# Spreading products for two token tiles at once, and a last norm in halves

## The chip, the cores and the metric

The kernel runs on one core of a Trainium2 chip. Its time is the device time of one execution in microseconds; several runs are taken, and their median counts.

## The reference

Two decoder layers on 1024 tokens (16 sequences of 64) of width 256. Each layer is self attention, cross attention, feed forward, each added to x and followed by a layer norm. Two places matter here. The first cross attention sees x and the context as 64 channels by 256 positions per sequence and has 8 heads of 8 channels with rotary angles:

```
q = _apply_rotary(q_emb, split_heads(_proj(x, Wq, bq)))
k = _apply_rotary(k_emb, split_heads(_proj(c, Wk, bk)))
scores = einsum('bhtc,bhsc->bhts', q, k) / sqrt(K_CH)
out = _proj(merge(einsum('bhts,bhsc->bhtc', softmax(scores), v)), Wo, bo)
```

and the very end is the last layer norm of the whole:

```
x = _layernorm(x + _L1_ffn_ref(x, ...))      # (x - mean) / sqrt(var + eps)
```

## The kernel before

All engines' instructions are written out by hand, each engine in its own program order, with semaphores between them (`wait_ge`, and `.by` to count up). x lies in SBUF as 8 tiles of 128 tokens (`NT = 8`, two sequences a tile), 256 columns each. PSUM is 8 banks of 512 columns.

**Spreading in the first cross attention.** For each tile u (0 to 7 are the keys, from the context; 8 to 15 the queries, from x) these steps follow each other:

1. `project(u)` on TensorE: one product of 256 columns into bank u % 2 (L799).
2. `rope_x(u)` on VectorE: adds the bias and multiplies with cosines and sines into `qr[:, u % 2]`, a buffer for two tiles (L2001). It waits until the spreading products of tile u-2 have read it.
3. `replicate(u)` on TensorE: spreads the 64 channels of both sequences of the tile (p = 0, 1) to 128 rows, for both halves of the heads (g = 0, 1), cosine and sine part (i = 0, 1). Each is a product of 64 rows by 128 columns, 256 columns moving, and f32, which the trace shows as two passes: 16 passes (L811). The two sequences stand in different row halves of the array.
4. `hi_part(u)` on ScalarE: two copies of a bank to f16 (L1634).
5. `stack_x(u)` on VectorE: two steps that put high and low parts into `stack`, f16 (L2009).

The bank of a product is chosen by sequence: banks 4 and 5 for all key tiles, 4 to 7 in turn for the queries. Thus for keys `replicate(u)` waits for `stack_x(u-1)`.

In the keys half TensorE also does the six large projections of the self attention (`project0`, 4 passes of 512 columns, L771) for tiles 0 to 5 and two value projections (`project_v0`, L781), and after it the value tiles of the cross attention (`values_in_x`, L826; j = 4 to 7 into banks 6 and 7, j = 0 to 3 into 4 and 5), the first scores (`scores0`, L838) and the memory products (`memory0`, L851) of the self attention. VectorE divides the latter (`memory_out0`, L2016, L2021), has the ELU steps (L2035, L2036) at tile 7, and then goes through the 16 softmax steps (L1978, L1979). ScalarE has `keep_v0` (L1645) and the bias step (L1661). After the norm of the self attention comes the queries half, with nothing but steps 1 to 5, and then the first score products (L938).

**The end.** The last feed forward runs in 16 half steps. Of each, TensorE's `outputs` sums down products into banks 4 to 7 (L1538, L1543, and, after VectorE's `down_ranks6`, L2503, the products L1547). After the last but one, tiles 0 to 3 are complete, after the last tiles 4 to 7. `take_sum(j)` adds tile j to x and takes its statistics (L2460, L1953, L1954). `normalise(6)` adds eps (L1958), waits for ScalarE's root (`ln_sqrt`, L1618), takes the reciprocal (L1960) and does 8 steps (L1962). SyncE then stores x with one DMA.

Of the kernel before, what the change touches and what calls it, by code (L numbers as in the profile page):

```python
# [13 lines left out]
ALU = mybir.AluOpType  # L14
# [3 lines left out]
P = 128  # L18
# [5 lines left out]
EPS = 1e-5  # L24
# [107 lines left out]
def build(nc, a):  # L132
    ctx = ExitStack()
    with ctx:
# [14 lines left out]
        def bank(i, n=1):  # L149
            return psum[:, i * BANK:(i + n) * BANK]  # L150
# [338 lines left out]
        sh_silu = again("sh_silu", otx_sb, B)  # L489
        mid_act = again("mid_act", elu_exp, 1)  # L490


# [29 lines left out]

        def replicated(u, p):
            return bank(4 + p if u < NT else 4 + 2 * (u % 2) + p)

# [3 lines left out]
        def _(sp):  # L529
# [72 lines left out]
            for f in range(FX):  # L602
# [13 lines left out]
                if f >= BUFS:  # L616
                    fetch_mix(f)
            sp.wait_ge(x_norm.sem, NT * 6)
            sp.dma_start(a["out"].rearrange("(j p) d -> p j d", p=P), x).then_inc(out_done.sem, 16)
            sp.wait_ge(out_done.sem, 16)  # L620

# [120 lines left out]
        def _(pe):  # L742
# [57 lines left out]

            def replicate(u):
                pe.wait_ge(qr_ready.sem, u + 1)
                for p in range(2):
                    back = 1 if u <= NT else 2
                    if u >= back:
                        pe.wait_ge(st_ready.sem, 2 * (u - back) + p + 1)
                for g in range(2):
                    for i, w in enumerate((c["rep"], c["rep_turned"])):
                        for p in range(2):
                            rows = slice(64 * p, 64 * p + 64)  # L810
                            last = pe.matmul(replicated(u, p)[:, g * D:(g + 1) * D], w[rows, g, :], qr[rows, u % 2, i, :],  # L811
                                             start=(i == 0), stop=(i == 1), tile_position=(64 * p, 0), skip_group_check=True)
                            if g == 1 and i == 1:
                                rep_ps.by(last)
# [85 lines left out]
            for j in range(NT // 2, NT):  # L900
                values_in_x(j)
            pe.wait_ge(vx_sb.sem, 1)
# [113 lines left out]
            for u in range(NT, 2 * NT + 1):  # L1016
                if u < 2 * NT:
                    project(u)
                if u > NT:
                    replicate(u - 1)  # L1020
            pe.wait_ge(st_ready.sem, 4 * NT)
# [583 lines left out]
        def _(act):  # L1605
# [22 lines left out]

            def hi_part(u):
                for p in range(2):  # L1630
                    act.wait_ge(rep_ps.sem, 2 * u + p + 1)
                    if u >= 2:
                        act.wait_ge(st_ready.sem, 2 * (u - 2) + p + 1)
                    hi_ready.by(act.activation(hi16[:, u % 2, p, :], replicated(u, p), ACT.Copy))  # L1634

# [14 lines left out]
            for u in range(NT + 1):  # L1650
                if u < 6:
                    keep_project0(u)
                if u >= 1:
                    hi_part(u - 1)
# [38 lines left out]

            for u in range(NT, 2 * NT):
                hi_part(u)

# [227 lines left out]
            for n in range(STEPS):  # L1924
                for i, (kind, src, dst) in enumerate((("g", slice(0, P), slice(0, P)),
# [4 lines left out]
                    else:  # L1930
                        act.wait_ge(sh_h.sem, sh_h.base + 2 * len(SHARED))
                    mid_act.by(act.activation(g6[dst, 2 * (n % 2) + i, :], bank(ring[(kind, 0), n] % 4)[src, :],  # L1932
                                              ACT.Silu))
            ln_sqrt(6)

        @block.vector
        def _(dve):
# [67 lines left out]
            def stack_x(u):  # L2005
                side, j = ("k", u) if u < NT else ("q", u - NT)
                for p in range(2):
                    dve.wait_ge(hi_ready.sem, 2 * u + p + 1)
                    do(dve.scalar_tensor_tensor(  # L2009
                        out=stack[side][:, 2 * j + p, :, :].rearrange("p a b -> p (a b)"), in0=hi16[:, u % 2, p, :],  # L2010
                        scalar=c["lo_" + side], in1=replicated(u, p), op0=ALU.mult, op1=ALU.add), st_ready)

# [15 lines left out]
            for u in range(NT + 1):  # L2028
                if u < NT:
                    rope_x(u)  # L2030
                if u >= 1:
                    stack_x(u - 1)
                if u == 7:
                    dve.wait_ge(elu_exp.sem, 1)
                    do(dve.tensor_scalar(sig0, sig0, 1.0, -1.0, ALU.min, ALU.add))  # L2035
                    do(dve.tensor_tensor(out=sig0, in0=q0, in1=sig0, op=ALU.max), elu_ready)  # L2036
            for m in range(2):
                memory_out0(m)
# [11 lines left out]

            for u in range(NT, 2 * NT + 1):
                if u < 2 * NT:
                    rope_x(u)
                if u > NT:
                    stack_x(u - 1)

# [452 lines left out]
            for step in range(-1, STEPS + 1):  # L2509
                if step + 1 < STEPS:  # L2510
                    inputs6(step + 1)
                if 0 <= step < STEPS:
                    hidden6(step, 0)
                if step + 1 < STEPS:
                    ranks6(step + 1)
                if 0 <= step < STEPS:
                    hidden6(step, 1)
                if step >= 1:
                    down_ranks6(step - 1)
                if step == STEPS - 1:  # L2520
                    for j in range(4):
                        take_sum(j)
            for j in range(4, NT):
                take_sum(j)
            normalise(6)

# [158 lines left out]
```

## Time and profile before

| what | us |
|---|---|
| median of 3 runs (1118.9 to 1127.76) | 1125.86 |
| the profiled execution, whole | 1121.06 |
| its span, first to last instruction | 1119.2 |
| TensorE busy | 976.2 (87%) |
| VectorE busy | 553.1 (49%) |
| ScalarE busy | 359.2 (32%) |
| mean granted TensorE clock | 0.927 |

The span is what the trace covers; 1.9 us of the execution lie around it. Matmuls are pipelined, so busy TensorE is not TensorE at its peak. PE is TensorE's matmuls, PEld its weight loads, DVE VectorE, ACT ScalarE, POOL GpSimd, SP SyncE.

### The profile page before, as it was taken

Reading aid. Unit: us, or ns where it says so; the run is one execution under the profiler, and the core shown is the slowest. Engines: PE = TensorE matmul, PEld = TensorE weight load, DVE = VectorE, ACT = ScalarE, POOL = GpSimd, SP = SyncE. Lnnn points to the kernel's source line nnn. Section 1 sums busy time; section 2 is a strip of 40 time slices with the busy share of each in tenths; the row PEclk is TensorE's granted clock in tenths of the full one; section 3 lists DMA queues with packets and bytes.
Section 4 is the critical chain, followed back from the end, with each engine's and each line's share of the span. In section 5 each row is a group of like instructions: output and inputs, shape, how many; then the busy total and the mean of one; then the engine's idle time right before and its main releaser. Section 6 shows DMA issues by size and latency. Waiting matters only on the chain.

```text
span 1119.2 us, 18944 instructions
## 1 busy us (share of the span) xinstructions
PE 976.2 (87%) x7488; PEld 610.2 (55%) x7488; DVE 553.1 (49%) x1113; ACT 359.2 (32%) x717; POOL 200.4 (18%) x241
## 2 busy tenths in 40 slices
PE   7998879997999999966773998889589999999994
PEld 4754523333478899953352667667454444444442
DVE  2699788885421111015687676457552323323325
ACT  3444246666222223322384443334211000000000
POOL 5011000000022222210037630060000111111110
PEclk9999869998899999987986999999578999999998
DMA  6000000000745555521001102030105022222001
GB/s 232 2 2 1 1 1 2 1 2 1 282 167 165 171 185 180 183 95 49 1 1 55 22 1 96 1 136 3 47 0 131 0 86 86 86 84 73 15 1 38
DMA packets 27210, 75.15 MB, mean 67 GB/s; under 512 B 9828, under 2 KB 17260, under 8 KB 21748
## 3 DMA queue, kind: packets, MB, share of 16 engines
q1 hardware_dynamic: 24916, 67.91, 18.1%
q0 software_dynamic: 2208, 6.03, 1.9%
q8 instruction: 61, 1.00, 0.4%
q14 instruction: 25, 0.20, 0.1%
HBM read 67.48 MB, written 6.46 MB: 66 GB/s over the span
## 4 chain that ended last, share of the span: by engine, by line
PE 70%; DVE 20%; issue 3%; ACT 3%; POOL 2%; DMA 2%; SPq 0%; DVEq 0%; POOLq 0%; ACTq 0%
PE psum L1513 8%; PE psum L1088 7%; PE psum L1100 7%; DVE arena L2060 4%; PE psum L811 3%; PE psum L1517 3%; PE psum L1279 3%; PE psum L1501 3%; PE psum L1543 2%; PE psum L1547 2%; PE psum L992 2%; PE psum L1479 2%; DVE arena L1979 2%; DVE arena L1978 2%; PE psum L1494 2%
## 5 line engine op out<-in xcount | busy, mean ns | idle before, releaser
L1513 PE MATMUL psum<-arena 128*128 128x512 f32 (+1 forms) x192 | 93.6, 625 | 0.5 <-DVE arena L2487 0.5
L1932 ACT ACTIVATE arena<-psum 128x512 f32<-128x512 f32 (+1 forms) x32 | 19.0, 593 | 227.3 <-PE psum L1517 227.3
L1752 ACT ACTIVATE arena<-psum,arena 128x128 f32<-128x128 f32 x184 | 52.6, 368 | 115.4 <-PE psum L1088 115.4
L2060 DVE TENSOR_REDUCE arena<-psum 128x2 f32<-128x512 f32 x128 | 82.6, 688 | 13.1 <-PE psum L938 11.0
L1088 PE MATMUL psum<-arena 128*128 128x128 f32 x736 | 86.7, 276 | 0.0
L737 POOL TENSOR_TENSOR arena<-arena 128x512 f32<-128x512 f32 (+1 forms) x32 | 40.5, 1265 | 257.2 <-ACT arena L1932 257.2
L1088 PEld LDWEIGHTS psum<-arena 128*128 128x128 f32 x736 | 84.0, 192 | 2.7 <-issue 2.7
L1100 PE MATMUL psum<-arena 128*128 x368 | 83.1, 379 | 0.0
L2207 DVE COPY arena<-psum 128x256 f32<-128x256 f32 x23 | 9.8, 425 | 136.2 <-PE psum L1073 85.8
L1729 ACT ACTIVATE arena<-psum 128x1024 f32<-128x1024 f32 x64 | 65.4, 1024 | 32.2 <-PE psum L960 29.0
L1100 PEld LDWEIGHTS psum<-arena 128*128 128x128 f32 x368 | 68.2, 190 | 8.4
L2487 DVE TENSOR_TENSOR arena<-arena,psum 128x512 f32<-128x512 f32 (+1 forms) x32 | 22.0, 688 | 90.0 <-POOL arena L737 89.5
L1513 PEld LDWEIGHTS psum<-arena 128*128 128x128 f32 (+1 forms) x192 | 34.2, 191 | 57.6 <-issue 55.9
L757 PE MATMUL psum<-arena 128*128 128x128 f32 x80 | 20.3, 401 | 44.2 <-DVE arena L1962 35.9
L938 PE MATMUL psum<-arena 32*128 32x256 f16 x256 | 47.8, 295 | 9.8 <-DVE arena L2060 4.3
L2470 DVE TENSOR_TENSOR arena<-psum,arena 128x512 f32<-128x512 f32 x32 | 22.1, 692 | 54.5 <-issue 45.8
L676 POOL DMA_INDIRECT returned<-arena x23 | 22.8, 990 | 123.1 <-DVE arena L2223 123.1
L685 POOL TENSOR_TENSOR arena<-arena 128x512 f32<-128x512 f32 x32 | 32.8, 1054 | 61.8 <-ACT arena L1792 43.7
L757 PEld LDWEIGHTS psum<-arena 128*128 128x128 f32 x80 | 11.5, 192 | 53.0 <-DVE arena L1962 40.6
L811 PE MATMUL psum<-arena 64*128 64x256 f32 x256 | 33.8, 404 | 3.8 <-DVE arena L2009 2.1
L992 PE MATMUL psum<-arena 128*32 128x256 f32 x512 | 36.0, 401 | 0.6 <-ACT arena L1729 0.5
L1517 PE MATMUL psum<-arena 64*128 64x512 f32 (+1 forms) x96 | 34.4, 625 | 0.0
(349 smaller groups left out, 1819.7 us busy)
## 6 DMA issues: line engine op xcount, KB each, us to landing
arena<-in_w SPq DMA_DIRECT2D x31, 1024.0 KB, 5.0
arena<-in_experts SPq DMA_DIRECT2D x8, 1248.0 KB, 5.9
arena<-mixed SPq DMA_DIRECT2D x16, 256.0 KB
arena<-mixed SPq DMA_DIRECT2D x8, 512.0 KB
arena<-in_ctx SPq DMA_DIRECT2D x2, 1024.0 KB, 7.1
arena<-returned SPq DMA_DIRECT2D x8, 256.0 KB, 4.6
arena<-in_w_xattn SPq DMA_DIRECT2D x1, 1538.5 KB, 10.0
arena<-in_w_ffn SPq DMA_DIRECT2D x1, 1152.0 KB, 5.2
```

What stands on the lines that cost most here:

```text
L737: do(pool.tensor_tensor(out=g6[rows, 2 * half + i, :], in0=g6[rows, 2 * half + i, :], in1=scale6[rows, f % BUFS, cols], op=ALU.mult), scaled6)
L811: last = pe.matmul(replicated(u, p)[:, g * D:(g + 1) * D], w[rows, g, :], qr[rows, u % 2, i, :], start=(i == 0), stop=(i == 1), tile_posit ...
L938: last = pe.matmul(bank(u % 2)[:, tc * D:(tc + 1) * D], stack["q"][r0:r1, b, g, tc * P:(tc + 1) * P], stack["k"][r0:r1, b, g, :], start=Tr ...
L992: last = pe.matmul(bank(6)[32 * q:32 * q + 32, 0:D], vx[:, b, sc, q, 32 * g:32 * g + 32], ptx[:, (n + q // 2) % 4, q % 2, sc, :], start=(g ...
L1088: last = pe.matmul(bank(n)[:, i * P:(i + 1) * P], w1_tile[:, r % 2, k, features], xst[:, r % 2, k, :], start=(k == 0), stop=(k == KC - 1))
L1100: last = pe.matmul(bank(4 + r % 2)[:, 0:D], hidt[:, r % 2, ic * P:(ic + 1) * P], w2v[:, bass.ds(e, 1), ic, :], start=(ic == 0), stop=(ic = ...
L1279: last = pe.matmul(bank(n % 4)[:, q * P:(q + 1) * P], lhs, xv1[rows, u, :], start=True, stop=True)
L1513: pe.matmul(out, e[w][:, k, :], xe6[:, half, k, :], start=(k == 0), stop=False)
L1517: mid_ps.by(pe.matmul(out, qb6[r0:r1, n // 2 % 2, q0:q0 + m], aw6[r0:r1, half, :], start=False, stop=True))
L1729: ptx_ready.by(act.activation(ptx[:, n % 4, :, :, :].rearrange("p a b c -> p (a b c)"), bank(2 + 2 * (n % 2), 2), ACT.Exp, scale=float(DHX ...
L1752: last = act.activation(hidt[:, r % 2, ic * P:(ic + 1) * P], bank(n)[:, i * P:(i + 1) * P], ACT.Gelu, bias=b1_tile[:, r % 4, ic:ic + 1])
L2060: ax_max.by(dve.tensor_reduce(nmx[:, b % 2, :, h], bank(u % 2).rearrange("p (t s) -> p t s", t=2), AX.X, ALU.max, negate=True))
```

## The change

The spreading products are done for two tiles at once. `replicate(m)` covers tiles 2m and 2m+1 with 512 moving columns, into bank 4 + 2g + p: four banks, by half of the heads and sequence. It runs when both tiles are roped; `rope_x(u)` of a following tile waits for the whole block before. `hi_part` and `stack_x` go by half of the heads; a stack step writes two runs of 256. All value tiles of the cross attention move behind the keys' last stack step. The last norm is done in two halves of four tiles: tiles 0 to 3 and 6, 7 are normalised on ScalarE with a scale and a shift, 4 and 5 on VectorE; `take_sum` of tiles 2 and 3 comes behind the last `down_ranks6`. The store is in three parts.

```diff
-        def replicated(u, p):
-            return bank(4 + p if u < NT else 4 + 2 * (u % 2) + p)
+        def replicated(g, p):
+            return bank(4 + 2 * g + p)
...
+            sp.wait_ge(x_act.sem, x_act.base + 4)
+            sp.dma_start(out_tiles[:, 0:4, :], x[:, 0:4, :]).then_inc(out_done.sem, 16)
+            sp.wait_ge(x_norm.sem, NT * 5 + 2)
+            sp.dma_start(out_tiles[:, 4:6, :], x[:, 4:6, :]).then_inc(out_done.sem, 16)
+            sp.wait_ge(x_act.sem, x_act.base + 6)
+            sp.dma_start(out_tiles[:, 6:8, :], x[:, 6:8, :]).then_inc(out_done.sem, 16)
...
+            def replicate(m):
+                pe.wait_ge(qr_ready.sem, 2 * m + 2)
                 for g in range(2):
+                    for p in range(2):
+                        if m >= 1:
+                            pe.wait_ge(st_ready.sem, 4 * (m - 1) + 2 * g + p + 1)
                     for i, w in enumerate((c["rep"], c["rep_turned"])):
                         for p in range(2):
                             rows = slice(64 * p, 64 * p + 64)
+                            last = pe.matmul(replicated(g, p).rearrange("p (u n) -> p u n", u=2), w[rows, g, :],
+                                             qr[rows, :, i, :], start=(i == 0), stop=(i == 1),
+                                             tile_position=(64 * p, 0), skip_group_check=True)
+                            if i == 1:
                                 rep_ps.by(last)
...
-                if u >= 1:
-                    replicate(u - 1)
+                if u >= 2 and u % 2 == 0:
+                    replicate(u // 2 - 1)
...
-            pe.wait_ge(qr_ready.sem, NT)
-            for j in range(NT // 2, NT):
-                values_in_x(j)
             pe.wait_ge(vx_sb.sem, 1)
             scores0(0)
             pe.wait_ge(v_sb.sem, 4)
             pe.wait_ge(elu_ready.sem, 1)
             memory0(0)
             memory0(1)
+            pe.wait_ge(st_ready.sem, 2 * NT)
+            for j in range(NT // 2, NT):
+                values_in_x(j)
+            for j in range(NT // 2):
+                values_in_x(j)
             pe.wait_ge(vx_sb.sem, 1 + NT // 2)
             memory0(2)
             memory0(3)
-            pe.wait_ge(st_ready.sem, 2 * NT)
-            for j in range(NT // 2):
-                values_in_x(j)
...
+            def hi_part(m):
+                for g in range(2):
+                    for p in range(2):
+                        act.wait_ge(rep_ps.sem, 4 * m + 2 * g + p + 1)
+                        if m >= 1:
+                            act.wait_ge(st_ready.sem, 4 * (m - 1) + 2 * g + p + 1)
+                        hi_ready.by(act.activation(hi16[:, g, p, :], replicated(g, p), ACT.Copy))
...
-            ln_sqrt(6)
+            def normalise_act(tiles):
+                act.wait_ge(less_mean6.sem, less_mean6.base + tiles[0] // 4 + 1)
+                for j in tiles:
+                    x_act.by(act.activation(x[:, j, :], x[:, j, :], ACT.Identity, scale=rstd[:, j:j + 1],
+                                            bias=shift6[:, j:j + 1]))
+
+            for j in range(0, NT, 4):
+                act.wait_ge(ln_var.sem, 7 + j // 4)
+                ln_std.by(act.activation(std[:, j:j + 4], rstd[:, j:j + 4], ACT.Sqrt))
+                normalise_act(range(j, 4) if j == 0 else range(6, NT))
...
                 if u >= 2:
-                    dve.wait_ge(rep_ps.sem, 2 * (u - 1))
+                    dve.wait_ge(rep_ps.sem, 4 * (u // 2))
...
-            for u in range(NT, 2 * NT + 1):
+            for u in range(NT, 2 * NT + 2):
                 if u < 2 * NT:
                     rope_x(u)
-                if u > NT:
-                    stack_x(u - 1)
+                if u >= NT + 2:
+                    stack_x(u // 2 - 1, u % 2)
...
+                if step == STEPS:
+                    for j in range(2):
+                        take_sum(j)
                 if step >= 1:
                     down_ranks6(step - 1)
-                if step == STEPS - 1:
-                    for j in range(4):
-                        take_sum(j)
...
+            for j in range(2, 4):
                 take_sum(j)
-            normalise(6)
+            add_eps(0)
+            take_sum(4)
+            scale_shift(0)
+            for j in range(5, NT):
+                take_sum(j)
+            add_eps(4)
+            scale_shift(4)
+            for j in range(4, 6):
+                x_norm.by(dve.tensor_scalar(x[:, j, :], x[:, j, :], mean_var[:, j, 0:1], rstd[:, j:j + 1],
+                                            ALU.subtract, ALU.mult))
```

`add_eps(j)` and `scale_shift(j)` are new: each works on columns j to j+3 of the tile statistics; the second takes the reciprocal of ScalarE's root and, in one step, minus mean times it, the shift.

## Rows read from the trace of the kernel before

**Rows 1.** The page's part 4: the chain that ended last, by engine.

```profile
PE 70%; DVE 20%; issue 3%; ACT 3%; POOL 2%; DMA 2%; SPq 0%; DVEq 0%; POOLq 0%; ACTq 0%
```

**Rows 2.** Chain of waits, keys half (start us, us, what).

```profile
14.20 1.72 PE psum L771 x4
...
25.06 2.00 PE psum L811 x16
...
27.07 1.91 PE psum L771 x4
```

**Rows 3.** TensorE timeline, 36-60 us (start, us, instruction, [idle before <-releaser]).

```profile
38.20 2.00 PE L811 MATMUL psum<-arena 64*128 64x256 f32 x16 [1.75 <-DVE arena L2009]
...
52.64 2.00 PE L851 MATMUL psum<-arena 64*128 64x65 f32 x32
...
54.47 2.00 PE L826 MATMUL psum<-arena 64*128 64x64 f32 x32
...
59.76 0.45 PE L838 MATMUL psum<-arena 32*64 32x256 f32 x4 [1.50 <-DVE arena L2021]
```

**Rows 4.** Timeline of all engines, 47 to 57 us.

```profile
47.07 1.23 DVE L2035 TENSOR_SCALAR arena<-arena 128x2048 f32<-128x2048 f32 x1
...
48.33 2.29 DVE L2036 TENSOR_TENSOR arena<-arena 128x2048 f32<-128x2048 f32 x1
...
49.19 1.09 ACT L1634 ACTIVATE arena<-psum 128x512 f16<-128x512 f32 x2 [2.44 <-PE psum L811]
...
51.30 0.26 ACT L1661 ACTIVATE arena<-psum,arena 128x1 f32<-128x1 f32 x1
...
56.19 1.23 DVE L1978 TENSOR_REDUCE arena<-psum 128x16 f32<-128x1024 f32 x1
```

**Rows 5.** Chain of waits, queries half.

```profile
117.84 3.79 PE psum L811 x16
...
127.84 1.93 PE psum L811 x16
...
129.77 0.63 PE psum L799 x2
```

**Rows 6.** Timeline of VectorE, queries half.

```profile
127.94 1.53 DVE L2009 SCALAR_TENSOR_TENSOR arena<-arena,psum 128x512 f16<-128x512 f16 x2 [0.24 <-ACT arena L1634]
...
129.51 0.75 DVE L2001 SCALAR_TENSOR_TENSOR arena<-psum,arena 128x512 f32<-128x512 f32 x1
```

**Rows 7.** Timeline of TensorE, the first score product.

```profile
142.67 0.40 PE L938 MATMUL psum<-arena 32*128 32x256 f16 x4 [2.67 <-DVE arena L2092]
```

**Rows 8.** Windows of 1 us (length, busy by engine, PEclk, DMA, GB/s).

```profile
61.00:62.00 1.00, 1.00 (x7) 1.00 (x6) 1.00 (x1) 0.00 (x0) 0.87 (x2) 0.54 0.00 0
...
122.00:123.00 1.00, 1.00 (x6) 0.39 (x7) 0.64 (x1) 0.74 (x2) 0.00 (x0) 0.74 0.00 0
...
143.00:144.00 1.00, 0.16 (x3) 0.10 (x2) 0.85 (x2) 0.00 (x0) 0.00 (x0) 0.50 0.00 0
```

**Rows 9.** Timeline of VectorE, the last 20 us.

```profile
1104.20 0.86 DVE L2503 TENSOR_TENSOR arena<-psum,arena 64x256 f32<-64x256 f32 x2
...
1106.36 0.42 DVE L2460 TENSOR_TENSOR arena<-psum,arena 128x256 f32<-128x256 f32 x1 [1.29 <-PE psum L1547]
...
1110.90 0.17 DVE L1958 TENSOR_SCALAR arena<-arena 128x8 f32<-128x8 f32 x1
...
1111.66 2.67 DVE L1962 TENSOR_SCALAR arena<-arena 128x256 f32<-128x256 f32 x8
```

**Rows 10.** Timeline of TensorE, its last work.

```profile
1105.12 1.99 PE L1547 MATMUL psum<-arena 128*128 128x256 f32 x8 [1.62 <-DVE arena L2503]
```

**Rows 11.** ScalarE's groups by shape (count | busy us, mean ns | idle before).

```profile
L1798 ACT ACTIVATE arena<-psum,arena 128x256 f32<-128x256 f32 x16 | 7.0, 510 | 0.0
```

**Rows 12.** The issues of DMA (count, KB each, us to landing).

```profile
out_x<-arena SPq DMA_DIRECT2D x1, 1024.0 KB, 4.5
...
arena<-in_w_route SPq DMA_DIRECT2D x1, 267.5 KB, 2.6
```

More of the change, by code:

```diff
@@ L490, in build @@
         mid_act = again("mid_act", elu_exp, 1)
+        x_act = again("x_act", x_beta, NT)
+        less_mean6 = again("less_mean6", kb5_ready, B)
+        shift6 = more6
         STEPS = 2 * FX
@@ L617, in _ @@
                     fetch_mix(f)
-            sp.wait_ge(x_norm.sem, NT * 6)
-            sp.dma_start(a["out"].rearrange("(j p) d -> p j d", p=P), x).then_inc(out_done.sem, 16)
-            sp.wait_ge(out_done.sem, 16)
+            out_tiles = a["out"].rearrange("(j p) d -> p j d", p=P)
+            sp.wait_ge(x_act.sem, x_act.base + 4)
[4 more added lines that the diff above has]
+            sp.dma_start(out_tiles[:, 6:8, :], x[:, 6:8, :]).then_inc(out_done.sem, 16)
+            sp.wait_ge(out_done.sem, 48)
         @block.gpsimd
@@ L799, in project @@
                 pj_ps.by(pe.matmul(bank(u % 2)[:, 0:D], x0["w" + side], src[:, j, :], start=True, stop=True))
[L801 to L806, printed above, removed]
+            def replicate(m):
+                pe.wait_ge(qr_ready.sem, 2 * m + 2)
                 for g in range(2):
+                    for p in range(2):
+                        if m >= 1:
+                            pe.wait_ge(st_ready.sem, 4 * (m - 1) + 2 * g + p + 1)
                     for i, w in enumerate((c["rep"], c["rep_turned"])):
@@ L810, in replicate @@
                             rows = slice(64 * p, 64 * p + 64)
-                            last = pe.matmul(replicated(u, p)[:, g * D:(g + 1) * D], w[rows, g, :], qr[rows, u % 2, i, :],
-                                             start=(i == 0), stop=(i == 1), tile_position=(64 * p, 0), skip_group_check=True)
-                            if g == 1 and i == 1:
+                            last = pe.matmul(replicated(g, p).rearrange("p (u n) -> p u n", u=2), w[rows, g, :],
+                                             qr[rows, :, i, :], start=(i == 0), stop=(i == 1),
+                                             tile_position=(64 * p, 0), skip_group_check=True)
+                            if i == 1:
                                 rep_ps.by(last)
@@ L1018, in _ @@
                     project(u)
-                if u > NT:
-                    replicate(u - 1)
+                if u > NT and u % 2 == 0:
+                    replicate(u // 2 - 1)
             pe.wait_ge(st_ready.sem, 4 * NT)
@@ L1652, in _ @@
                     keep_project0(u)
-                if u >= 1:
-                    hi_part(u - 1)
+                if u >= 2 and u % 2 == 0:
+                    hi_part(u // 2 - 1)
                 if u == 6:
@@ L1691, in _ @@
             ln_sqrt(0)
-            for u in range(NT, 2 * NT):
-                hi_part(u)
+            for m in range(NT // 2, NT):
+                hi_part(m)
             def copy_max(b):
@@ L2003, in rope_x, with stack_x @@
                                             op0=ALU.add, op1=ALU.mult), qr_ready)
-            def stack_x(u):
-                side, j = ("k", u) if u < NT else ("q", u - NT)
+            def stack_x(m, g):
+                side, j = ("k", 2 * m) if m < NT // 2 else ("q", 2 * m - NT)
                 for p in range(2):
-                    dve.wait_ge(hi_ready.sem, 2 * u + p + 1)
+                    dve.wait_ge(hi_ready.sem, 4 * m + 2 * g + p + 1)
                     do(dve.scalar_tensor_tensor(
-                        out=stack[side][:, 2 * j + p, :, :].rearrange("p a b -> p (a b)"), in0=hi16[:, u % 2, p, :],
-                        scalar=c["lo_" + side], in1=replicated(u, p), op0=ALU.mult, op1=ALU.add), st_ready)
+                        out=stack[side][:, 2 * j + p:2 * j + p + 3:2, g, :],
+                        in0=hi16[:, g, p, :].rearrange("p (u n) -> p u n", u=2),
+                        scalar=c["lo_" + side], in1=replicated(g, p).rearrange("p (u n) -> p u n", u=2),
+                        op0=ALU.mult, op1=ALU.add), st_ready)
             def memory_out0(m):
@@ L2030, in _ @@
                     rope_x(u)
-                if u >= 1:
-                    stack_x(u - 1)
+                if u >= 2:
+                    stack_x(u // 2 - 1, u % 2)
                 if u == 7:
@@ L2036, in _ @@
                     do(dve.tensor_tensor(out=sig0, in0=q0, in1=sig0, op=ALU.max), elu_ready)
+            stack_x(NT // 2 - 1, 1)
             for m in range(2):
@@ L2517, in _, with add_eps, scale_shift @@
                     hidden6(step, 1)
+                if step == STEPS:
+                    for j in range(2):
+                        take_sum(j)
                 if step >= 1:
                     down_ranks6(step - 1)
-                if step == STEPS - 1:
-                    for j in range(4):
-                        take_sum(j)
-            for j in range(4, NT):
-                take_sum(j)
-            normalise(6)
+            def add_eps(j):
+                do(dve.tensor_scalar(rstd[:, j:j + 4], mean_var[:, j:j + 4, 1], EPS, None, ALU.add), ln_var)
+            def scale_shift(j):
+                dve.wait_ge(ln_std.sem, 7 + j // 4)
+                do(dve.reciprocal(rstd[:, j:j + 4], std[:, j:j + 4]))
+                do(dve.scalar_tensor_tensor(out=shift6[:, j:j + 4], in0=mean_var[:, j:j + 4, 0], scalar=-1.0,
+                                            in1=rstd[:, j:j + 4], op0=ALU.mult, op1=ALU.mult), less_mean6)
+            for j in range(2, 4):
+                take_sum(j)
+            add_eps(0)
[8 more added lines that the diff above has]
+                                            ALU.subtract, ALU.mult))
         for name, s in renamed:
```

9 lines of the change are left out of this document (1 added, 8 removed).

## The prediction

> **What bounds the kernel now.** I read the page first: of the chain that ended last, 70% is TensorE and 20% VectorE [rows 1]. That says only that small DMA or ScalarE savings are worth nothing unless they lie on this chain, so each edited place was then read alone, in the chain of waits and the timelines of its engines. There are three places: the keys half of the spreading work (16 to 56 us), its queries half (115 to 143 us), and the last 20 us.
>
> In the keys half TensorE has the bound. One token tile costs it one full-array projection for the self attention, 1.91 us, one small projection, and one block of spreading products, 2.00 us [rows 2]. From tile 5 on, where the large projections have run out, it also waits for VectorE's stack step, 1.75 us at 38.20 [rows 3]. In the queries half nothing else is left for TensorE to do: spreading 1.93 us plus small projection 0.63 us make a period of 2.56 us [rows 5], while VectorE needs 1.53 us for two stack steps and 0.75 us for the rope step, 2.3 us [rows 6]. TensorE bounds it, and VectorE is only 0.25 us behind. At the end VectorE has the bound: sums, statistics, norm; then one store [rows 9, 12].
>
> **Part 1, what a block for two tiles costs.** Before, a tile took 16 matmul passes of 256 columns in 1.93 us, so a pair of passes in the two row halves takes 0.241 us. A full-array pass of 512 columns takes 1.72/4 = 0.43 us [rows 2] and one of 256 columns half of that, 0.215, so the overhead of a row-tiled pair is 0.026 us. The new block has 16 passes of 512 columns: 8 x (0.43 + 0.026) = 3.65 us against 3.86 for two old blocks. Bounds: with no overhead 8 x 0.43 = 3.44; with no gain, twice the steady 2.00 [rows 2], 4.00. I take 3.65, since nothing in the rows lets a pair be shorter than its columns. Stack and rope steps keep their elements and their number (32 and 16). The stack's output is now two runs of 256 instead of one of 512; no row shows that, I cost it at nothing, at most 0.1 us a step.
>
> **Part 2, what the two-tile block waits for.** The buffer of roped tiles holds two tiles. Before, the rope step of tile u waited for the block of tile u-2, so one tile was being spread while the next was roped. Now one block reads both halves, so no rope step for the next pair can start before it has ended, and the next block waits for both. On VectorE, in program order, stand between the two blocks: rope, two stack steps, rope, that is 0.75 + 1.53 + 0.75 and some 0.18 of hand-over (0.03 between own steps, 0.05 to 0.07 between engines) = 3.2 us. The stack steps of the second half of heads come after that and are ready before the block's second half needs them (1.55 us against 1.83).
>
> **Keys half.** That gap of 3.2 us is covered as long as TensorE has other work behind the block. From 16.35 on (14.20 + 1.72 and a small projection of 0.43 [rows 2]), the order is: projection 1.72, small 0.43, block 0, to 22.2; projection 1.91, small, projection 1.72, small (4.5 us, cover complete), block 1 from 26.7 to 30.4; projection, two small ones (2.8 us, 0.45 short), block 2 from 33.65 to 37.35; value projection 2.0, small, value projection 2.0 (cover complete), block 3 from 42.05 to 45.75. Before, the eighth block ended at 49.18, where ScalarE took it up [rows 4]. That is 3.4 us later, but the gain isn't kept. The ELU steps (1.23 and 2.29 us) stand on VectorE ahead of the last pair's two stack rounds [rows 4], so these (rope step 7 from 40.0 on, two stack steps, then ELU, 5.85 us with hand-over) begin at 45.85 and end at 45.85 + 4 x 0.77 = 48.95. ScalarE's last copies of the block (1.09 from its end), keep_v0 (1.0) and the bias step (0.26) end at 48.15. Before, the bias step ended at 51.56 and the first four value tiles of the cross attention ran in its shadow, since they used banks that the keys half left free. Now the spreading uses those banks too, and all value tiles wait for the last stack step and stand in one row: scores 1.09 and two memory products 1.0 to 50.35, values 2 x 2.0 to 54.4, memory products 2 and 3 to 55.5 [rows 3], VectorE's second memory_out to 56.5. Only then comes the first softmax, which began at 56.19 [rows 4]. **Term: +0.4 us.** Bounds: -1.2 with the shorter block in all four places (-0.8) and values at 1.8 us as the second group ran; +1.8 with 4.00. From there to 114 us VectorE has the bound and the shift passes through.
>
> **Queries half.** Here is no cover. The first block waits for project(10) too, which the new order puts ahead of it: the clock is low there (the old block took 3.79 us [rows 5]), the product costs 1.1 us from 117.84, so the block starts at 119.0 rather than 117.84. The clock rose at about 122.26 (mean 0.74 in the slice of 122 [rows 8]); till then 3.26 us do 1.63 us of work, the rest takes 2.0: end at 124.3. Then three rounds of 3.2 + 3.65 = 6.85 us, against 2 x 2.56 = 5.12 before: end at 144.9. Behind the last block stand, as before, 2.67 us up to the first score product [rows 7], here one half of the heads rather than one tile, the same four instructions. First score at 147.5 instead of 142.67. **Term: +4.8 us.** Bounds: 3.44 gives 4.0, 4.00 gives 6.1.
>
> **Tail.** In the old order VectorE does four sums (the four later ones: 1106.36 to 1110.90, 1.135 each), only then the rank products of the last half step (0.86), and TensorE stood idle 1.62 us for these, VectorE then 1.29 for TensorE [rows 9, 10]. With the rank products after two sums they end at 1102.8, TensorE goes on at once at 1103.5, and its first two tiles are there at 1104.7. VectorE reaches sum 4 at 1105.3, so both waits are gone: -1.29. Added on VectorE's row are a 4-column add, a reciprocal and a shift for the first half: 0.19 + 0.23 + 0.22 = +0.64. Last sum ends at 1110.90 - 1.29 + 0.64 = 1110.25. Then add 0.19, root 0.31 with its hand-over, reciprocal 0.23, shift 0.22: 1111.2. The old eight norm steps took 2.67 [rows 9]. Of the new ones four run on ScalarE from 1106.9 on, hidden behind sums 5 to 7 (4 x 0.51 = 2.0 [rows 11], end at 1109); two on VectorE, 0.67, end at 1111.9; two on ScalarE, 2 x 0.51 by the row of a 128x256 step with a scale operand, end at 1112.3. (0.4 to 0.8 each: 1112.0 to 1112.9.) SyncE gives out the last 256 KB at about 1112.4. The old 1 MB was given out when the last norm step ended, 1114.33, and landed 4.5 us later [rows 9, 12]; a load of 267.5 KB in the same queue landed after 2.6 [rows 12]. End at 1115.0 instead of 1118.9. **Term: -3.8 us**, bounds -3.0 and -4.6.
>
> **Sum.** +0.4 + 4.8 - 3.8 = +1.4 us. On the profiled execution (1121.06 us, of it 1119.2 span) that gives 1122.5; the median of the three runs, 1125.86, lies 4.8 above it, and I put the sum on that: **1127.3 us**. The bounds of the terms together are -1.8 and +4.9.
>
> **A rule of the skill, and the trace.** In the rows the block behind a TensorE pause of 1.75 us, at 38.20, took 2.00 us like those before it, so the clock had stayed at its upper level of 2.4 GHz [rows 2, 3], while one of 1.50 us at 59.76 was followed by a fall to half, 1.2 GHz, at 61, and one of 2.67 us at 142.67 by a fall at 143 [rows 3, 7, 8]. The queries half gets three pauses of 3.2 us, filled only by two small projections (about 1.1 us). The Trainium skill ("TensorE: Matmul & The Clock Gate", section "A second HAM failure mode: psum-queue depth-cycling") says that an engine that pauses shortly between groups of matmuls as it goes through its banks swings between both clocks and loses throughput. By that rule the low clock costs up to another 3.65 us in each of the three blocks; by the row at 38.20 it costs nothing. What each would give is rival B.
>
> **The rivals.**
> A. The early end of the keys half is kept: if the value tiles were not the last to arrive, the first softmax would start up to 3.4 us earlier and the total would be -3.4 + 4.8 - 3.8 = -2.4: 1123.5. For it: the eighth block is 3.4 us earlier. Against: 4 us of value products now stand in series behind the last stack step.
> B. The clock falls in the pauses of the queries half, **slower than before**: if one block runs at the low clock, the sum is +1.4 + 3.65 = +5.1, 1131; if all three do, and the first one's tail as well, +1.4 + 11 + 2 = +14, 1140. It decides from the point at which a pause of about 2 us between dense blocks is enough for a fall; two rows of short pauses speak on either side.
> C. The queries half doesn't serialise as I say, or the new block is much shorter than its columns: the term falls to about 0 and the tail remains, -3.4: 1122.5. Against: program order and the two-tile buffer leave no freedom.
> D. The change doesn't do what it says at the end: the store's landing is set by something else than its size, so that the three stores end 4.5 us after the last issue: +3.3, 1129.
>
> **How the numbers follow.** Forecast 0.60, A 0.10, B 0.17 (0.04 of it the full case), C 0.06, D 0.07. A measurement of this kernel can tell about 1%, 11 us. Only the full case of B passes it, besides what chance in the place of the clock's falls elsewhere may add, for which I leave 0.02 on either side. Faster by over 1% 0.02, within 1% 0.92, slower 0.06. The range: from C and A, 1122 and 1123, less 2 for the spread of the runs (1118.9 to 1127.76), to B with one or two low blocks: 1120 to 1133.
>
> **What would show it.** The two-tile block at 3.65 us; in the queries half TensorE idle some 2 us ahead of each block, released by the rope step, with periods of 6.85 us; the first score product 4 to 6 us later than before relative to the end of the norm; the first softmax near 56.5 us; the last sum followed by 4.5 to 5 us to the end instead of 8. I am wrong if the block takes under 3.2 or over 4.2 us, if the granted clock falls between 124 and 145 us, if ScalarE's norm steps or the last store end later than 1116, or if a shift of the stages moves the clock's falls in the score stage (143 to 160 us, half clock), worth 1 to 3 us either way.

## The result and the profile after

The changed kernel has a median of 1133.28 us over 11 runs, the kernel before 1125.86 over 11. The ratio is 1.0081, 95% interval 1.0050 to 1.0112: slower by 0.8%, less than the 1% that I had set, but clear of noise. The forecast was 1127.3 us. One of the eleven executions took 2805.19 us, with a granted clock of 1.0, and stands apart from the other ten (1126.66 to 1138.6); the ratio is without it. The changed kernel's profiled execution took 1130.41 us with a span of 1128.6, so 9.4 more than the 1119.2 of before. Five stretches of the two traces, cut at the same instruction in each, add up to that:

| stretch | before | after | difference | forecast |
|---|---|---|---|---|
| start to the first softmax step | 56.19 | 60.86 | +4.67 | +0.4 |
| to the first step of the first norm | 58.14 | 59.12 | +0.98 | 0 |
| to the first score product | 28.34 | 35.42 | +7.08 | +4.8 |
| to the rank products of the last but one half step | 954.83 | 955.43 | +0.6 | 0 |
| to the end of the span | 21.7 | 17.77 | -3.93 | -3.8 |

The tail came as forecast, the queries half mostly, the keys half not at all. That the fourth stretch, which no edit touches, gives only +0.6 is a balance of larger differences (see the end). TensorE in the keys half, from its timeline in the trace after (start, us, instruction, idle time before it and what ended it):

```profile
33.52 3.70 PE L818 MATMUL psum<-arena 64*128 64x512 f32 x16 [0.56 <-DVE arena L2019]
...
41.80 3.71 PE L818 MATMUL psum<-arena 64*128 64x512 f32 x16
...
47.95 1.09 PE L846 MATMUL psum<-arena 32*64 32x256 f32 x16 [2.23 <-ACT arena L1669]
48.98 1.74 PE L859 MATMUL psum<-arena 64*128 64x65 f32 x16
50.50 7.09 PE L834 MATMUL psum<-arena 64*128 64x64 f32 x64
57.32 5.53 PE L859 MATMUL psum<-arena 64*128 64x65 f32 x48
```

The answers to [rows 2, 3]. The block for two tiles takes 3.70 us; 3.65 was forecast, and the old pair of blocks took 4.0. The fourth block ends at 45.4, forecast 45.75. Up to there all is as worked out. Then TensorE waits 2.23 us for ScalarE's bias step (L1669), and what follows runs at half speed: the 64 passes of the value tiles take 7.09 us, where 32 took 2.0 before [rows 3]. The windows of the same kernel (length, busy by engine, granted clock, DMA) say why:

```profile
30.00:45.00 15.00, 14.44 (x172) 8.57 (x170) 11.64 (x14) 7.57 (x12) 0.00 (x0) 1.00 0.01 2
45.00:48.00 3.00, 0.77 (x12) 0.24 (x8) 2.89 (x4) 2.29 (x5) 0.00 (x0) 1.00 0.00 0
49.00:60.00 11.00, 11.00 (x110) 11.00 (x107) 1.14 (x5) 2.42 (x8) 1.23 (x2) 0.51 0.01 2
60.00:70.00 10.00, 8.43 (x67) 5.78 (x65) 7.61 (x13) 1.02 (x1) 3.65 (x6) 0.51 0.00 1
```

TensorE had been busy 0.77 us of the 3 from 45, and its clock stood at 0.51, the 1.2 GHz level, from 49 to 70. VectorE, from its timeline, waits 8.00 us for the memory products behind the value tiles (L859), and the softmax (L1996) begins at 60.86:

```profile
59.82 0.21 DVE L2036 RECIPROCAL arena<-psum 128x8 f32<-128x8 f32 x1 [8.00 <-PE psum L859]
60.06 0.76 DVE L2041 TENSOR_TENSOR arena<-psum,arena 128x256 f32<-128x256 f32 x2
60.86 1.22 DVE L1996 TENSOR_REDUCE arena<-psum 128x16 f32<-128x1024 f32 x1
```

The queries half, TensorE's timeline, answers to [rows 5]:

```profile
124.70 5.21 PE L818 MATMUL psum<-arena 64*128 64x512 f32 x16
129.85 0.70 PE L807 MATMUL psum<-arena 128*128 128x256 f32 x2
130.99 0.67 PE L807 MATMUL psum<-arena 128*128 128x256 f32 x2 [0.45 <-DVE arena L2019]
133.26 3.70 PE L818 MATMUL psum<-arena 64*128 64x512 f32 x16 [1.59 <-DVE arena L2019]
136.89 0.70 PE L807 MATMUL psum<-arena 128*128 128x256 f32 x2
138.03 0.67 PE L807 MATMUL psum<-arena 128*128 128x256 f32 x2 [0.44 <-DVE arena L2019]
140.29 3.71 PE L818 MATMUL psum<-arena 64*128 64x512 f32 x16 [1.59 <-DVE arena L2019]
143.93 0.70 PE L807 MATMUL psum<-arena 128*128 128x256 f32 x2
147.33 5.40 PE L818 MATMUL psum<-arena 64*128 64x512 f32 x16 [2.70 <-DVE arena L2019]
```

Blocks start every 7.04 us (133.26, 140.29, 147.33), 6.85 forecast, and what TensorE waits for is each time the rope step (L2019). VectorE between two blocks is the sequence of the forecast, rope, two stack steps, rope:

```profile
137.13 0.75 DVE L2019 SCALAR_TENSOR_TENSOR arena<-psum,arena 128x512 f32<-128x512 f32 x1 [2.37 <-PE psum L818]
137.92 1.53 DVE L2027 SCALAR_TENSOR_TENSOR arena<-arena,psum 128x512 f16<-128x512 f16 x2
139.49 0.75 DVE L2019 SCALAR_TENSOR_TENSOR arena<-psum,arena 128x512 f32<-128x512 f32 x1
```

The last block took 5.40 us: behind the 2.70 us pause the clock fell at 148 (0.55 in the window from 149 to 152). It doesn't in every execution, as the experiments show.

The end, timelines of VectorE, ScalarE and SyncE, then the issues of DMA, answers to [rows 9, 10, 12]:

```profile
1115.26 0.86 DVE L2524 TENSOR_TENSOR arena<-psum,arena 64x256 f32<-64x256 f32 x2
...
1123.59 0.17 DVE L2546 TENSOR_SCALAR arena<-arena 128x4 f32<-128x4 f32 x1
...
1124.51 0.73 DVE L2564 TENSOR_SCALAR arena<-arena 128x256 f32<-128x256 f32 x2
```

```profile
1120.18 2.07 ACT L1946 ACTIVATE arena<-arena 128x256 f32<-128x256 f32 x4 [1.34 <-DVE arena L2551]
...
1124.51 1.09 ACT L1946 ACTIVATE arena<-arena 128x256 f32<-128x256 f32 x2 [0.51 <-DVE arena L2551]
```

```profile
1125.72 0.47 SPq L627 DMA_DIRECT2D out_x<-arena  x1
```

```profile
out_x<-arena SPq DMA_DIRECT2D x1, 512.0 KB, 2.9
out_x<-arena SPq DMA_DIRECT2D x2, 256.0 KB, 2.3
```

Four norm steps on ScalarE are over before the last sums; the last pair ends at 1125.6, 0.4 us after VectorE's. The two stores of 256 KB land 2.3 us after their issue (the median of the two), the old 1 MB took 4.5.

### The profile page after: what moved, and what is told of

It reads as the page before. It is cut to its first block, busy times and chain, and to the rows that moved or that the text cites. A ratio compares the mean times of both kernels' runs of the same rounds, so it can differ in the third digit from the quotient of the medians.

```text
span 1128.6 us, 18694 instructions
## 1 busy us (share of the span) xinstructions
PE 984.0 (87%) x7360; PEld 606.2 (54%) x7360; DVE 551.9 (49%) x1111; ACT 362.4 (32%) x724; POOL 200.1 (18%) x241
## 4 chain that ended last, share of the span: by engine, by line
PE 71%; DVE 21%; issue 3%; ACT 2%; DMA 2%; POOL 0%; SPq 0%; DVEq 0%; ACTq 0%; POOLq 0%
PE psum L1520 8%; PE psum L1095 7%; PE psum L1107 7%; DVE arena L2081 4%; PE psum L818 3%; PE psum L1524 3%; PE psum L1286 3%; PE psum L1550 3%; PE psum L1508 3%; PE psum L1554 2%; PE psum L999 2%; DVE arena L1997 2%; DVE arena L1996 2%; PE psum L1545 2%; PE psum L1486 2%
## 5 line engine op out<-in xcount | busy, mean ns | idle before, releaser
L945 PE MATMUL psum<-arena 32*128 32x256 f16 x256 | 47.9, 300 | 9.9 <-DVE arena L2081 4.5
L818 PE MATMUL psum<-arena 64*128 64x512 f32 x128 | 32.8, 655 | 6.4 <-DVE arena L2019 6.4
```

The costliest lines, as they stand in the source:

```text
L818: last = pe.matmul(replicated(g, p).rearrange("p (u n) -> p u n", u=2), w[rows, g, :], qr[rows, :, i, :], start=(i == 0), stop=(i == 1), t ...
L945: last = pe.matmul(bank(u % 2)[:, tc * D:(tc + 1) * D], stack["q"][r0:r1, b, g, tc * P:(tc + 1) * P], stack["k"][r0:r1, b, g, :], start=Tr ...
```

## The experiments

Each ratio is to the kernel before, run on the same chip in the same rounds. "First softmax", "first norm" and "first score" are the start times of the steps that cut the table above, in that kernel's profiled execution, one for each kernel.

| kernel | ratio, 95% interval | first softmax | first norm | norm to first score |
|---|---|---|---|---|
| before | 1 | 56.19 | 114.33 | 28.34 |
| changed | 1.0081 (1.0050 to 1.0112) | 60.86 | 119.98 | 35.42 |
| tail alone | 0.9987 (0.9951 to 1.0022) | 56.12 | 114.31 | 28.08 |
| keys alone | 1.0094 (1.0056 to 1.0131) | 62.17 | 121.45 | 28.40 |
| queries alone | 1.0093 (1.0059 to 1.0126) | 56.76 | 113.88 | 34.67 |
| changed, five fillers | 1.0079 (1.0049 to 1.0110) | 59.37 | 117.42 | 34.85 |
| changed, two fillers | 1.0010 (0.9982 to 1.0038) | 56.00 | 115.27 | 35.85 |
| two fillers, queries filled too | 0.9998 (0.9968 to 1.0029) | 57.47 | 116.52 | 33.69 |
| changed, four buffers | 0.9966 (0.9935 to 0.9997) | 62.19 | 121.45 | 28.55 |
| before, tail, softmax first | 0.9945 (0.9913 to 0.9978) | 53.59 | 112.97 | 27.92 |
| four buffers, two fillers, softmax first | 0.9959 (0.9936 to 0.9983) | * | 110.39 | 28.80 |
| four buffers, pause closed, softmax first | 0.9944 (0.9917 to 0.9972) | * | 111.64 | 29.25 |
| changed, pause closed | 1.0031 (1.0003 to 1.0059) | 55.88 | 115.14 | 35.64 |

(*: the early softmax runs at 49, before the memory steps; it isn't comparable.)

**The three places one at a time.** The tail alone is the diff's last part (SyncE, `normalise_act`, `add_eps`, `scale_shift`, the order of `take_sum`) on the kernel before.

> The kernel before with the new last norm and store alone. Theory (each of the three places acts by itself): the stretch from VectorE's rank products of the last but one half step to the end shrinks from 20.8 to 16.9 us, nothing else changes: -3.9 us against the kernel before. Rival (the store's landing or the clock elsewhere eats it): under 1 us gained.

From the last but one rank products to the end 17.8 us, as in the changed kernel: the tail's gain is there in full, -3.9. The ratio, 0.9987, allows -5.5 to +2.5 us, so by time alone it is only not contradicted.

The keys alone keep `replicate(m)` for tiles 0 to 7 and go by tile from 8 on, and the queries alone the reverse; both have the old tail:

```diff
-                if u > NT and u % 2 == 0:
-                    replicate(u // 2 - 1)
+                if u > NT:
+                    replicate_one(u - 1)
```

> Two-tile blocks for the keys alone, queries tile by tile, old tail. Theory: TensorE's pause of 2.2 us at 45.5 us lets the clock fall at about 48, the value and memory products then run at half clock, the first softmax starts at about 60.9 instead of 56.2: +4 to +5 us against the kernel before; the queries half keeps its 28.3 us from the end of the statistics to the first score product. Rival (the keys half is neutral as forecast, the shift comes from the queries): first softmax at 56.5, total +0.4.

> Two-tile blocks for the queries alone, keys and value tiles in the old order, old tail. Theory: from the first norm step to the first score product 33 us with the clock up throughout, 35.4 with a clock fall in a pause, instead of 28.3: +4.8 to +7 us against the kernel before. Rival (the rope steps overlap in some way): under +1 us.

With the keys alone the first softmax starts 6.0 us late and the queries half keeps its length, 28.40; with the queries alone the first softmax is within 0.6 us of where it was and the queries half grows by 6.3. So the two losses are separate. Both hold the theory and fell the rivals as far as stages go. The keys alone lose 1.3 us more than the same code in the changed kernel, mostly since the clock fell 1.4 us sooner (at 47.9, ahead of the first scores, which took 1.98 us instead of 1.09). The ratios (+10 us each) are larger than the stages, and all three together make 1.0175 where the whole change has 1.0081. With the queries alone the rest lies in code that no edit touches: the stretch from the second norm to the last but one rank products took 828.6 us, in the kernel before 820.4. With the keys alone it took 821.1 in the profiled execution, 1129.70 us, which is shorter than most of that kernel's (median 1133.53); where its other executions lose the rest isn't shown.

**Is it the clock, in the keys half?** The changed kernel, with products that nobody reads in TensorE's pause of 2.23 us:

```diff
+            for k in range(5):
+                pe.matmul(bank(1), a0["wk"][:, k % KC, :], xt[:, k % KC, 0:BANK], start=True, stop=True)
             pe.wait_ge(vx_sb.sem, 1)
             scores0(0)
```

> The changed kernel with five more products of 512 columns (2.15 us at full clock) into a free bank of PSUM, in TensorE's pause of 2.2 us between the last keys block and the first scores. They compute nothing that is read. Theory (the clock's fall in that pause makes the keys half late): the granted clock stays up at 48 us, value products take 4.0 us instead of 7.1, the first softmax starts at 56.5 instead of 60.9, total -4 us against the changed kernel. Rival (the order of the value tiles makes it late, with either clock): first softmax still at 60 to 61, total unchanged or up to +0.5.

It was mis-sized: f32 products go in two passes, so five lasted 4.5 us and put the first scores off from 47.95 to 51.16. Still the clock stayed up to 62 and the value tiles took 3.8 us; the first softmax was 1.5 us earlier than in the changed kernel, not 4.4, and the ratio, 1.0079, gained nothing. With two:

```diff
-            for k in range(5):
+            for k in range(2):
```

> As the kernel with five filling products, but with two (each is two passes in f32, so five lasted 4.5 us in a pause of 2.2 and pushed the first scores back by 2.2 us; two last 1.7 us). Theory: the clock stays up at 48 us, the first scores start at 48 as in the changed kernel, the first softmax at 57 (59.37 less 2.2) instead of 60.86. Rival (the long row of value products makes it late at any clock): 60 or later.

TensorE's timeline of this kernel, then its windows:

```profile
45.49 1.99 PE L908 MATMUL psum<-arena 128*128 128x512 f32 x4
47.80 1.09 PE L846 MATMUL psum<-arena 32*64 32x256 f32 x16 [0.32 <-ACT arena L1671]
48.82 1.11 PE L859 MATMUL psum<-arena 64*128 64x65 f32 x16
49.77 3.79 PE L834 MATMUL psum<-arena 64*128 64x64 f32 x64
```

```profile
49.00:60.00 11.00, 7.88 (x132) 7.48 (x136) 5.75 (x13) 2.43 (x8) 3.19 (x6) 0.96 0.01 3
```

TensorE does more work here than in the changed kernel and waits for the same ScalarE step; the value tiles take 3.79 us instead of 7.09, and the first softmax starts at 56.00, 4.9 us earlier, in fact where it was before the change. This is the experiment that settles the keys half: the pause cost nothing by its length, it cost the clock behind it. The ratio agrees, 1.0010 with an interval that doesn't touch the changed kernel's. Nor is it the luck of one trace: in all three kernels with the open pause of 2.23 us (changed, keys alone, four buffers) the clock fell at 48 to 49 and the first softmax came at 60.86 to 62.19; in none of the four with products in the pause did it fall before 59. With the two fillers the first softmax came at 56.00 and, with the same code up to there, at 57.47. The rival, the row of value tiles as such, is not to be seen beside that: the code of before gives 56.12 to 56.76 in three kernels. The same pause closed with the kernel's own work, by moving `output_bias_x`, the bias step and the last `keep_v0` ahead of the last block and starting four value tiles after the first stack round:

```diff
+                if u == NT:
+                    output_bias_x()
                 if u >= 2 and u % 2 == 0:
                     replicate(u // 2 - 1)
...
-            pe.wait_ge(st_ready.sem, 2 * NT)
-            for j in range(NT // 2, NT):
-                values_in_x(j)
+            pe.wait_ge(st_ready.sem, 2 * NT - 2)
             for j in range(NT // 2):
                 values_in_x(j)
+            pe.wait_ge(st_ready.sem, 2 * NT)
+            for j in range(NT // 2, NT):
+                values_in_x(j)
```

> The changed kernel with its keys pause closed by its own work alone (no filling products, two buffers, softmax at its old place). Theory: clock up at 48 us, value products 3.6 instead of 7.1 us, first softmax at 54.5 to 56 instead of 60.9, ratio to the kernel before about 1.000 as with two filling products. Rival (filling products helped by something else than the absence of a pause): clock falls at 47 to 49 as before, softmax at 59 or later.

TensorE's timeline:

```profile
46.15 1.09 PE L846 MATMUL psum<-arena 32*64 32x256 f32 x16
47.18 1.11 PE L859 MATMUL psum<-arena 64*128 64x65 f32 x16
48.12 3.79 PE L834 MATMUL psum<-arena 64*128 64x64 f32 x64
53.21 2.00 PE L859 MATMUL psum<-arena 64*128 64x65 f32 x32 [1.30 <-ACT arena L1679]
```

(The second memory products now wait until all eight value tiles are copied, which is the pause of 1.30 us.) First softmax at 55.88, as with the fillers. The clock did fall, but at 55, behind that pause, when the value tiles were done. Its ratio, 1.0031, is a little above the forecast of 1.000; the stages don't show why.

**The queries half: clock or order?** One more product ahead of each block, two ahead of the last, besides the two in the keys pause:

```diff
+                    if u > NT + 2:
+                        for k in range(1 if u < 2 * NT else 2):
+                            pe.matmul(bank(2), x0["wq"], ctok.rearrange("p j d -> p (j d)")[:, 0:BANK], start=True, stop=True)
                     replicate(u // 2 - 1)
```

> The changed kernel with the two filling products in the keys pause and, in the queries half, one product of 512 columns (two passes, 0.86 us) ahead of the blocks of 3.7 us in the pauses of 1.6 us, and two in the pause of 2.7 us; nothing reads them. Theory (the queries half is late by its program order, not by its clock): the period of 7.04 us stays, from the first norm step to the first score product 34 to 35 us (35.4 in the changed kernel, whose last block alone ran at half clock). Rival (the pauses' clock falls are the main cost there): near 30 us.

The period stayed at 7.04 (blocks at 129.77, 136.80, 143.84). From the first norm to the first score it took 33.69 us, a little under the 34 to 35 expected and instead of 35.42; the last block took 3.70 us instead of 5.40, which makes the clock's part 1.7 us. That the filling kept the clock up isn't shown, because two kernels without filling in the queries half have the same pause and the same block, and no fall. TensorE's timelines of the queries alone and of the changed kernel with five fillers in the keys half:

```profile
142.17 3.71 PE L813 MATMUL psum<-arena 64*128 64x512 f32 x16 [2.70 <-DVE arena L2027]
```

```profile
145.89 3.70 PE L818 MATMUL psum<-arena 64*128 64x512 f32 x16 [2.70 <-DVE arena L2021]
```

In the changed kernel, with two fillers and with the keys pause closed the block took 5.40 us. So the 1.7 us come in some executions. The other 5.3 us are the order, which the next kernel takes away:

```diff
-        qr = arena.take(2, 2, D)
+        qr = arena.take(4, 2, D)
...
-                if u >= 2:
-                    dve.wait_ge(rep_ps.sem, 4 * (u // 2))
+                if u >= 4:
+                    dve.wait_ge(rep_ps.sem, 4 * (u // 2 - 1))
```

> The changed kernel with a buffer of four roped tiles instead of two, so that a rope step waits for the block before the last one. Theory: the queries period falls from 7.04 to about 5.3 us (3.7 block, 0.63 small product, 0.8 rope step, hand-over), from the first norm step to the first score product 29.5 to 30.5 us instead of 35.4, total -5 us against the changed kernel. Rival (TensorE's pauses come from the stack steps, not from the buffer): period stays at 7.

TensorE's timeline:

```profile
133.16 3.71 PE L818 MATMUL psum<-arena 64*128 64x512 f32 x16 [0.47 <-DVE arena L2019]
136.79 1.13 PE L807 MATMUL psum<-arena 128*128 128x256 f32 x4
138.39 3.71 PE L818 MATMUL psum<-arena 64*128 64x512 f32 x16 [0.47 <-DVE arena L2019]
```

A period of 5.23 us, 28.55 from norm to first score (29.5 to 30.5 expected): all 7 us are won back, and no more, since 5.23 for two tiles is no better than 2 x 2.56 of before. The keys half of this kernel still had its fall (0.90 in the window of 47, 0.50 in that of 48) and its first softmax at 62.19; yet its ratio is 0.9966.

**A version that beats both.** VectorE idles while TensorE makes the memory products, although the first scores are there. On the kernel before with the new tail:

```diff
+            softmax0(0)
             for m in range(2):
                 memory_out0(m)
-            softmax0(0)
```

> The kernel before with the new tail, and with VectorE's first softmax ahead of its first two memory steps (a version meant to beat both). Theory: the first softmax starts at about 52.8 instead of 56.2, in VectorE's pause, the first norm 1.5 us earlier, tail -3.9 us: total -5 us against the kernel before, ratio 0.995. Rival (the memory products behind it become late and the gain is lost by the second softmax): ratio as with the tail alone, 0.9987.

0.9945 (0.9913 to 0.9978), first softmax at 53.59, first norm 1.4 us earlier. The forecast was 52.8 and 1.5. The two-tile blocks with all cures together, the edits shown above and the early softmax, once with the fillers and once with the pause closed by own work, are no better:

> The changed kernel with four roped-tile buffers, the two filling products in the keys pause, and VectorE's first softmax ahead of its first two memory steps. Theory (the two losses are separate, so their cures add up): keys clock up at 48 us, first softmax at about 51, first norm near 113, from there 28.5 us to the first score product, tail 17.8 us: ratio to the kernel before 0.988, faster than any kernel so far. Rival (the cures share their gain, or the clock falls elsewhere instead): 0.995 or more.

> As the kernel with four buffers, filling products and the early softmax, but the keys pause is closed with the kernel's own work and no filling: the bias product and step and the last keep_v0 go ahead of the last block, the value tiles of the first half of the heads' banks start after the first stack round. Theory: the first scores start right behind the last block at 45.6 us, the clock stays up, ratio 0.986 to 0.989. Rival (a pause further back, near 52 us, drops the clock instead): first norm later by 2 us or more than with the filling.

0.9959 and 0.9944. By stages the cures do add up: the first norm starts at 110.39 and 111.64, 3.9 and 2.7 us ahead of the kernel before. But at the first score product, at 139.19 and 140.89, they are only 1.7 and 0 us ahead of the simple version (140.89), since their queries half takes 28.80 and 29.25 us, there 27.92. So the stages promise no more than the totals show. For both, the 0.986 to 0.989 that I expected was too much; I had added up ratios that carried some us of unchanged code. A pause near 52 us did drop the clock in the second of the two, as its rival had it, and its first norm was 1.25 us later than with fillers.

## Why the prediction was wrong

**The step that failed is the keys term**, +0.4 with bounds of -1.2 and +1.8 (by its own parts the lower one is 0.4 - 0.8 - 0.4 = -0.8). It had every wait in its place: fourth block to 45.75 (45.4), ScalarE's bias step to 48.15 (47.9), first scores then. It priced all that follows (scores, two memory products, value tiles 2 x 2.0, memory products) from rows at full clock, though it had just put a TensorE pause of 2.4 us ahead of them, longer than the 1.50 us pause at 59.76 that I quoted as one after which the clock fell. Measured: +4.67, with the clock at half from 49 to 70. With the pause filled or closed this is gone (56.00 and 55.88). The +0.98 on the way to the first norm is not: with two fillers that stretch takes 59.27 us, with the pause closed 59.26, before 58.14. There the clock fell anew, from 59 to 66 with two fillers, where it was low from 61 to 64.5 before, and with the queries alone, where it didn't fall there, the stretch took 57.12. The sentence "the shift passes through" had no clock in it either. Rival B had the mechanism, but in the wrong place: I looked for pauses only in the queries half, and the bounds of the keys term had no clock in them.

**The queries term** was right in mechanism: the order rope, two stack steps, rope between blocks, shown by four buffers. It was short by 2.3 us (+7.08 against +4.8): 1.7 for one block at low clock, which is rival B's first case with half its price, since only part of the block was affected, and 0.6 for three periods of 7.04 rather than 6.85 us. The 1.7 came in three of the five kernels with that pause. The first block's 5.21 us (5.3 forecast) have luck in them as well: in the two kernels whose last block kept its clock it took 6.16 and 6.33, the clock having risen later.

**The block's own price** (3.70 against 3.65) and **the tail** (-3.93 against -3.8, landing 2.3 against 2.6) were right. Rivals A and C are out: the early end of the keys blocks was not kept, and the queries did serialise. D is out by the landing of the parts.

**What the Trainium skill says of short pauses** ("TensorE: Matmul & The Clock Gate", section "A second HAM failure mode: psum-queue depth-cycling"), that they make the clock swing, agrees with the trace for the keys pause of 2.23 us. For the last queries pause of 2.70 us it agrees in three kernels of five. It doesn't for the pauses of 1.59 us between dense blocks, behind which blocks took 3.70 us in all of these five. The row at 38.20 had told me the latter rightly, and I let it stand for all pauses.

Of the +7.4 us between the medians the stages named give +8.8 in the profiled pair; that the two agree so well is partly luck, see below.

## What to carry to other kernels

When you work out a pause of TensorE, price what comes behind it at both clocks before you use it; a pause that is off the critical path by its length can still put the next 20 us at half speed. Doing two tiles per block needs four tiles of buffer, else the double buffering that was there is gone: count, for the new unit, how many units the buffer holds. Don't judge a pause by one trace, since the clock fell behind the same pause in one kernel's execution and not in another's. And where a change ends some engine's work earlier, ask who has to wait for the last of it anyway.

## What the runs showed beside that

- The clock fell behind pauses of very different length: 1.30 us (at 52, fall at 55), 1.50 us [rows 3], 2.23 us and 2.70 us. Pauses of 1.59 us between blocks with all rows in use did nothing in five kernels. Neither length nor the work around a pause decides alone: the 2.70 us pause in the queries half stands between the same blocks in five kernels and was followed by a fall in three. The one of 1.50 us of [rows 3] is there with the queries alone as well (1.51 us, at 60.33), and there the granted clock stayed at 1.00 from 55 to 70.
- Code that no kernel here touched took different times. From the first step of the norm ahead of the last feed forward to its last but one rank products it was 302.3 us before, 302.1 with the tail alone, 301.3 with the queries alone, 299.7 with the queries filled too, and 295.5 after, with the keys alone and in the simple early softmax version. The trace says where that arises. TensorE was busy 292.98 of the 302.3 us at a mean granted clock of 0.93, and 286.21 of the 295.5 at 0.96; VectorE's busy time is the same (97.39 and 97.41 us). The two differences, 6.8 us each, are one: the same work at a lower clock. What makes the clock fall more often there isn't shown.
- The spread of one kernel follows the clock too: of 35 executions of the kernel before, the fastest, 1118.06 us, had a mean granted clock of 0.933, the slowest, 1131.84, one of 0.914. So one profiled pair can differ by 7 us for no reason in the change, as much as this change costs; the stages' own lengths and medians of 10 or more runs were needed together.
